# A transformer block on one core: chunk 0's first norm moved to ACT and POOL, and the last r and v products in high and low parts

## The reference

```python
x = x + attn(layernorm(x))        # causal linear attention, 16 heads of 16, features elu + 1
x = x + ffn(layernorm(x))
# attn: q = a @ Wq + bq; k, v = (a @ Wk + bk) @ Wc @ We, ...; o = num / den;
#       y = a + o @ Wo + bo;  return norm(y) * gamma + beta
# ffn:  xr = mu_r*x + (1-mu_r)*x_prev;  xk = mu_k*x + (1-mu_k)*x_prev
#       r = sigmoid(xr @ W_r);  k = xk @ W_k;  return r * (square(relu(k)) @ W_v)
```

## Time and profile before

| | us |
|---|---|
| median of 3 runs | 290.19 |
| lowest, highest | 287.93, 290.63 |
| profiled execution | 290.58 |
| its span, first to last instruction | 288.8 |
| PE busy | 264.8 (92%) |
| DVE busy | 225.1 (78%) |
| ACT busy | 154.1 (53%) |
| POOL busy | 127.3 (44%) |

### The profile page before, as it was taken

One profiled execution on the slowest core, in us unless ns is written; L12 is line 12 of the kernel. 1 busy time (PEld: TensorE's weight loads), 2 busy tenths in 40 slices (PEclk: granted clock), 3 DMA queues, 4 the chain that ended last, 5 costly groups with the idle time before them and its releaser, 6 DMA issues.

```text
span 288.8 us, 7520 instructions
## 1 busy us (share of the span) xinstructions
PE 264.8 (92%) x2961; PEld 190.6 (66%) x2961; DVE 225.1 (78%) x550; ACT 154.1 (53%) x312; POOL 127.3 (44%) x151
## 2 busy tenths in 40 slices
PE   7886988983899999999999999999999999989794
PEld 6755656742685588757885588558855767766563
DVE  6587487969597979977997989796979758977523
ACT  2384684480643866388456854586248630453540
POOL 2628423100983358515853576355543514051510
PEclk9998999996599999999999999999999999999999
DMA  7900120000020003000400020001000020000312
GB/s 195 265 19 11 65 76 3 2 0 2 4 72 0 2 24 123 2 5 2 145 2 2 0 76 2 0 2 64 13 2 3 1 74 2 0 2 1 109 36 73
DMA packets 12178, 10.73 MB, mean 37 GB/s; under 512 B 2288, under 2 KB 12144, under 8 KB 12144
## 3 DMA queue, kind: packets, MB, share of 16 engines
q1 hardware_dynamic: 11392, 9.97, 11.1%
q10 hardware_dynamic: 752, 0.30, 0.4%
HBM read 6.07 MB, written 4.19 MB: 36 GB/s over the span
## 4 chain that ended last, share of the span: by engine, by line
PE 77%; DVE 11%; ACT 5%; issue 3%; DMA 2%; POOL 1%; ACTq 0%; DVEq 0%; POOLq 0%
PE ps_x L461 10%; PE ps_x L381 9%; PE ps_z L432 6%; PE ps_x L476 6%; PE ps_x L483 6%; PE ps_x L375 6%; PE ps_y L448 5%; PE ps_y L453 5%; PE ps_x L501 4%; PE ps_x L469 3%; PE ps_z L476 3%; PE ps_z L483 2%; DVE probs L991 2%; PE ps_x L368 2%; PE ps_z L415 2%
## 5 line engine op out<-in xcount | busy, mean ns | idle before, releaser
L991 DVE TENSOR_TENSOR probs<-ps_z,causal 128x1024 f32<-128x1024 f32 x32 | 38.7, 1211 | 6.3 <-PE ps_z L432 5.5
L461 PE MATMUL ps_x<-wo_sb,oT 128*128 128x256 f32 x128 | 29.6, 382 | 0.0
L381 PE MATMUL ps_x<-aT,wq_sb 128*128 128x512 f32 x60 | 27.8, 604 | 0.0
L278 POOL TENSOR_TENSOR out_tok<-tanh_r,x_tok 128x512 f32<-128x512 f32 x14 | 17.8, 1275 | 21.9 <-DVE tanh_r L1064 20.9
L461 PEld LDWEIGHTS ps_x<-wo_sb,oT 128*128 128x128 f32 x128 | 23.6, 190 | 3.8 <-issue 0.9
L248 POOL TENSOR_TENSOR abo_tok<-a_tok,bo_bc 128x1024 f32<-128x1024 f32 x8 | 18.9, 2361 | 16.3 <-issue 5.6
L255 POOL TENSOR_TENSOR xb_tok<-x_in,beta_bc 128x1024 f32<-128x1024 f32 x8 | 18.9, 2356 | 16.0 <-DVE x_tok L1037 16.0
L218 POOL TENSOR_TENSOR rstd<-rstd,neg_half 128x4 f32<-128x4 f32 x24 | 24.9, 1038 | 1.9
L448 PE MATMUL ps_y<-qf,state 32*32 32x128 f32 x512 | 20.9, 278 | 5.3 <-DVE oT L1005 4.7
L432 PE MATMUL ps_z<-qf,kfT 32*128 32x128 f32 x512 | 24.1, 304 | 1.4 <-ACT rden_bc L711 0.5
L263 POOL TENSOR_TENSOR prod<-qf,ksum 128x1024 f32<-128x1024 f32 x5 | 11.8, 2361 | 29.9 <-DVE ksum L962 29.9
(11 more groups left out here) (144 smaller groups left out, 623.6 us busy)
## 6 DMA issues: line engine op xcount, KB each, us to landing
x_in<-in_L_attn_x_dram SPq DMA_DIRECT2D x8, 512.0 KB, 4.2
out_dram<-out_tok SPq DMA_DIRECT2D x16, 256.0 KB, 2.1
xr<-in_L_attn_Wq_dram ACTq DMA_DIRECT2D x1, 256.0 KB, 4.0
xk<-in_L_ffn_W_r_dram SPq DMA_DIRECT2D x1, 256.0 KB, 4.8
xk<-in_L_ffn_W_k_dram SPq DMA_DIRECT2D x1, 256.0 KB, 5.0
xr<-in_L_ffn_W_v_dram SPq DMA_DIRECT2D x1, 256.0 KB, 5.5
wo_sb<-in_L_attn_Wo_dram SPq DMA_DIRECT2D x4, 64.0 KB, 5.0
bo_bc<-in_L_attn_bo_dram SPq DMA_DIRECT2D x1, 128.0 KB, 5.0
```

Of the source, the lines that this page charges most:

```text
L278: PL.tensor_tensor(out_tok[:, 2 * i:2 * i + 2, :], tanh_r[:, i].rearrange("p (b d) -> p b d", b=2), x2_tok[m % 3][:, 2 * i:2 * i + 2, :], ...
L381: last = mm(bk_[:, :], wq_sb[:, k, a, :], aT[:, k, :], start=(k == 0), stop=(k == KD - 1))
L461: last = mm(bk_[:, (b % 2) * D:(b % 2 + 1) * D], oT[m % 2][:, a, b, :], wo_sb[:, a, :], start=(a == 0), stop=(a == 1))
L991: V.tensor_tensor(probs[b % 2][:].rearrange("p g (r s) -> p g r s", s=HALF), ps_z[:, :, 0:2 * P].rearrange("p g (r s) -> p g r s", s=HALF) ...
```

## The change

In the first short steps:

- `denominator_terms` goes from DVE to POOL for chunks 1 and 2 (DVE keeps chunk 0's, as `prepare_denominators`), and PE's `denominators` and `outputs(c, 3)` change places.
- Chunk 0's `centre` and `second_residual` leave DVE. POOL makes `rstd1` and `nbias1`, ACT's `normalise_y` scales y in place, and POOL's `scale_residual` multiplies by gamma and adds `xb_tok`, eight operations of 128 x 256. DVE takes chunk 0's second statistics in two halves.
- POOL's `second_norm` and `add_beta` change places, and PE's wait for the reciprocal at the head of a step becomes a wait for `s_den`, the operation before it.

In the finale, r and v of chunks 5, 6 and 7 are made from parts. ACT makes the high parts (`high_xr`, and `channel_k` with its last argument true), POOL the low ones (`low_xr`, `low_ka`), and PE calls `mix_r_parts` and `mix_v_parts`. The weight `wrT` is split once, in step 0. DVE's `second_residual(7)` goes behind the two r shifts of chunk 6.

```diff
+            def scale_residual(m):
+                for b in range(NB + 1):
+                    if b < NB:
+                        pool.wait_ge(s_n1, b + 1)
+                        PL.tensor_tensor(y_tok[:, b, :], y_tok[:, b, :], gamma_bc[:], ALU.mult).then_inc(s_t, 1)
+                    if b:
+                        pool.wait_ge(s_t, b)
+                        PL.tensor_tensor(x2_tok[m % 3][:, b - 1, :], y_tok[:, b - 1, :], xb_tok[m % 2][:, b - 1, :],
+                                         ALU.add).then_inc(s_x2, 1)
...
+            def low_parts(parts, whole, high, value, done):
+                for k in range(KD):
+                    pool.wait_ge(high, value + k + 1)
+                    PL.tensor_tensor(flat(parts[1])[:, k * T:(k + 1) * T], whole(k),
+                                     flat(parts[0])[:, k * T:(k + 1) * T].bitcast(F32), ALU.subtract).then_inc(done, 1)
...
                     if m >= 0:
-                        first_norm(m)
-                        second_norm(m)
+                        scale_and_bias(m, mv1, neg_mean1, rstd1, nbias1, s_st1, s_rs1, s_nb1)
+                        scale_residual(m)
                     else:
                         pool.wait_ge(s_kf, 2 * n + 2)
                     add_bo(n)
-                    add_beta(n)
                     if m < 0:
+                        add_beta(n)
+                        pool.wait_ge(wr_split, 1)
+                        PL.tensor_tensor(wr_p[1][:], wrT[:], wr_p[0][:].bitcast(F32), ALU.subtract).then_inc(wr_split, 1)
+                    denominator_terms(n)
+                    if m >= 0:
+                        second_norm(m)
+                        add_beta(n)
+                    else:
                         pool.wait_ge(wv_split, 1)
                         PL.tensor_tensor(wv_p[1][:], wvT[:], wv_p[0][:].bitcast(F32), ALU.subtract).then_inc(wv_split, 1)
                 if f >= 0:
...
+            def low_xr(m):
+                pool.wait_ge(s_r_ps, 2 * m)
+                low_parts(xr_p, lambda k: xr[:, k].rearrange("p b t -> p (b t)"), s_xrh, 2 * (m - FIRST), s_xrl)
+
+            def low_ka(m):
+                pool.wait_ge(s_v_ps, 2 * m)
+                low_parts(ka_p, lambda k: k_act[:, k, :], s_kah, 2 * m, s_kal)
...
                 m, f = c - 1, c - 2
                 token_difference(f)
                 first_norm(m)
+                low_xr(f)
                 second_norm(m)
+                low_ka(f)
                 first_norm(c)
                 token_difference(m)
+                low_xr(m)
                 second_norm(c)
+                low_ka(m)
                 finish(f)
+                low_xr(c)
                 finish(m)
+                low_ka(c)
...
+            def mix_r_parts(m, i, bk_):
+                pe.wait_ge(s_xrh, 2 * (m - FIRST) + 2)
+                for b in (2 * i, 2 * i + 1):
+                    out = bk_[:, (b % 2) * D:(b % 2 + 1) * D]
+                    for k in range(KD):
+                        for part in range(2):
+                            mm(out, xr_p[0][:, k, b * P:(b + 1) * P], wr_p[part][:, k, :], start=(k == 0 and part == 0), stop=False)
+                    if b == 0:
+                        pe.wait_ge(s_xrl, 2 * (m - FIRST) + 2)
+                    for k in range(KD):
+                        last = mm(out, xr_p[1][:, k, b * P:(b + 1) * P], wr_p[0][:, k, :], start=False, stop=(k == KD - 1))
+                last.then_inc(s_r_ps, 1)
...
                     if m < 0:
                         pe.wait_ge(ffn_w_sb, 2)
                         ffn_weight(2, x1)
-                denominators(n)
+                if f >= 0:
+                    denominators(n)
                 outputs(c, 3)
+                if f < 0:
+                    denominators(n)
                 if f >= 0:
                     pe.wait_ge(wv_split, 2)
...
                 out_projection(c, 1, x0)
                 mix_k(f, 1, z1)
-                mix_r(f, 0, z2)
-                mix_r(f, 1, z3)
+                mix_r_parts(f, 0, z2)
+                mix_r_parts(f, 1, z3)
                 pe.wait_ge(s_zT, 2 * f + 2)
-                mix_v(f, 0, x1)
+                mix_v_parts(f, 0, x1)
                 pe.wait_ge(s_y, 2 * c + 2)
                 transpose_z(m, x0, x2)
                 pe.wait_ge(s_oT, 4 * c + 4)
-                mix_v(f, 1, ps_y)
+                mix_v_parts(f, 1, ps_y)
...
+            def normalise_y(m):
+                act.wait_ge(s_nb1, 2 * m + 2)
+                for b in range(NB):
+                    AC.activation(y_tok[:, b, :], y_tok[:, b, :], ACT.Identity, bias=nbias1[:, b:b + 1],
+                                  scale=rstd1[:, b:b + 1]).then_inc(s_n1, 1)
...
+            def high_part(parts, whole, ready, value, done, ks=range(KD)):
+                for k in ks:
+                    act.wait_ge(ready, value + k + 1)
+                    copy(flat(parts[0])[:, k * T:(k + 1) * T], whole(k)).then_inc(done, 1)
...
                 if f >= 0:
                     gate_r(f, 0, x1)
+                if c == 1:
+                    normalise_y(m)
                 double_keys(n)
+                if c == 0:
+                    act.wait_ge(ffn_w_sb, 1)
+                    copy(flat(wr_p[0]), flat(wrT)).then_inc(wr_split, 1)
...
+            def high_xr(m):
+                act.wait_ge(s_r_ps, 2 * m)
+                high_part(xr_p, lambda k: xr[:, k].rearrange("p b t -> p (b t)"), s_xr, 2 * m, s_xrh)
+
             def finale(c):
                 m, f = c - 1, c - 2
                 act.wait_ge(s_rb_ps, c + 1)
@@ -855,20 +927,23 @@
                 for b, bk_ in ((0, ps_y), (1, x2), (2, x0), (3, x1)):
                     copy(rden_bc[c % 2][:, b].rearrange("p a t -> p (a t)"), bk_[:, 0:2 * P]).then_inc(s_rb, 1)
                 shift_z(f, x0, x1)
-                channel_k(f, 0, z0)
-                channel_k(f, 1, z1)
+                high_xr(f)
+                channel_k(f, 0, z0, True)
+                channel_k(f, 1, z1, True)
                 gate_r(f, 0, z2)
                 gate_r(f, 1, z3)
                 normalise_z(m)
                 shift_z(m, x0, x2)
-                channel_k(m, 0, z0)
-                channel_k(m, 1, z1)
+                high_xr(m)
+                channel_k(m, 0, z0, True)
+                channel_k(m, 1, z1, True)
                 normalise_z(c)
...
-            def second_stats(m):
+            def second_stats(m, rows=range(NB)):
                 if m >= 1:
                     dve.wait_ge(s_nb2, 2 * m)
-                dve.wait_ge(s_x2, 4 * m + 4)
-                row_stats(x2_tok[m % 3], stats2, s_st2, 8 * m, range(NB))
-                row_means(stats2, mv2, s_st2, 8 * m)
+                dve.wait_ge(s_x2, 4 * m + rows[-1] + 1)
+                row_stats(x2_tok[m % 3], stats2, s_st2, 8 * m, rows)
+                if rows[-1] == NB - 1:
+                    row_means(stats2, mv2, s_st2, 8 * m)
...
                 divide(c, 0)
                 mask(c, 2)
                 queries(n, 0, x0)
+                if m >= 0:
+                    second_stats(m, (0, 1))
                 queries(n, 1, x1)
                 divide(c, 1)
                 states(n)
                 key_sums(n)
-                denominator_terms(n)
                 mask(c, 3)
-                if m >= 0:
-                    centre(m)
-                    second_residual(m)
                 divide(c, 2)
                 if m >= 0:
-                    second_stats(m)
+                    second_stats(m, (2, 3))
...
                 gate(f, 1, ps_y)
                 token_shift(m, 0, *for_k)
                 token_shift(m, 1, *for_k)
-                second_residual(c)
                 token_shift(m, 0, *for_r)
                 token_shift(m, 1, *for_r)
+                second_residual(c)
                 second_stats(c)
```

53 lines of the change are left out of this document (26 added, 27 removed).

## The result

| us | before | after |
|---|---|---|
| median (lowest to highest), 4 runs each | 290.22 (287.93 to 290.63) | 295.25 (294.17 to 296.25) |
| profiled execution | 290.58 | 296.17 |
| its span | 288.8 | 294.4 |
| ratio after/before, 95% interval | | 1.0184 (1.0121 to 1.0246) |

The account below looks back on a forecast made before the run. PE bounds 90 to 230 us outright, with free time in the second short step and the finale. Forecast: 290.6 − 5.0 (front) + 10.9 (finale) = 296.5, 296.1 as median, since the profiled execution lies 0.4 over it; range 288.0 to 300.5.

Parts of the forecast that it names:

- length 1, clock falls / stays: Step c=1's reciprocal spread to step c=2's output projection: 4.2 us off if PE's clock falls, 5.9 if not.
- PE idle at v(5): Finale, chunk 5: after four high products of v, PE waits 4.0 us for POOL's low ka.
- mix_k(6), mix_k(7) from the finale's start: Finale: PE starts these calls for chunks 6 and 7 later than before, by 5.6 and 10.2 us.
- finale, clock down / up in the gaps: Finale's added time: 11.6 us if PE's clock falls in its gaps, 9.2 if it stays up; 10.9 taken.
- The front: First short steps, chunk 0's first norm off DVE: earlier output projection, 5.0 us off, ends 4.2 and 5.9.
- the replay: Finale worked through on the earlier trace's times: stretched residual, late statistics, POOL's queue, PE gaps, clock fall; end +11.6 us.
- PE's own saving: Finale: twelve r and v calls in parts, 1.44 us each for 1.73, save 3.5 us of PE.
- B: Rival, finale: the parts stay hidden and the finale saves its 3.5 us, total 280.8; chance 0.08.
- C: Rival, finale: POOL and DVE do not hinder each other, PE gaps of 2.4 us, total 288.4; chance 0.20.
- D: Rival, finale: clock also falls before mix_k, so mix_k(6) and (7) run at 1.2 GHz, 299.7; 0.15 with E.
- E: Rival, front: POOL's 256-column operations cost 1.27 us, about half the front's gain goes, total 299; 0.15 with D.
- length 0: From the start to the spread of the reciprocals in step c=1; the forecast's sum has no term for it.

Follow-up runs that it names:

- front_only: Changed kernel with the finale's r and v back as float32 products, so only the first steps are changed: 283.01 us, ratio 0.9762 to the kernel before.
- tail_parts_dve: Changed kernel with only r and v of chunk 7 in parts, their low parts on DVE, the rest float32: 284.42 us, ratio 0.9831.
- experiment 3: Also spelled low_xr_after_x2: changed kernel with POOL's low parts of xr(5) and xr(6) waiting until the next chunk's second_residual is done: 290.0 us, ratio 1.0016.
- v_parts_only: Changed kernel with r of chunks 5 to 7 as float32 products, only v in parts: 288.7 us, ratio 0.9953.
- lows_on_dve: Changed kernel with all low parts of the finale, chunks 5 to 7, on DVE and none on POOL: 287.97 us, ratio 0.9944.
- tail_and_filler: tail_parts_dve with twenty unused products on PE in the gaps of steps 0, 1 and 2: 282.77 us, ratio 0.9768.
- finale_only: Changed kernel with the first steps of the kernel before (wrT still split), so only the finale is changed: 301.46 us, ratio 1.0427.
- r_parts_only: Changed kernel with v of chunks 5 to 7 as float32 products, only r in parts: 288.52 us, ratio 0.9927.
- late_parts_dve: Changed kernel with only v(6), r(7) and v(7) in parts, their low parts on DVE, the rest float32: 285.79 us, ratio 0.9861.

## Why the prediction was right

| step | forecast | measured |
|---|---|---|
| POOL's 128x256 operation | 0.73, pitch 0.68 | 0.73, pitch 0.69 |
| length 1, clock falls / stays | −4.2 / −5.9, taken −5.0 | −4.70 / −6.14 |
| `second_residual(6)` | 3.97 | 3.71 |
| PE idle at v(5) | 4.0 | 3.79, then 3.77 at v(6) |
| the other eight products of v's first call | 1.7 | 1.06, then 1.87 |
| z transposes behind it | 2.0 | 1.83 and 1.66 |
| mix_k(6), mix_k(7) from the finale's start | +5.6, +10.2 | +4.76, +9.00 |
| finale, clock down / up in the gaps | +11.6 / +9.2, taken +10.9 | +11.87 / +9.19 |

**The front** came as worked out, with its clock: the taken −5.0 lies between its two ends, and both ends were seen, in the changed kernel and in front_only, 0.2 to 0.5 us better than forecast each.

**The finale** followed the replay, every link of it: the stretched residual, the late statistics, the queue on POOL, the gap, the clock. The replay was 0.8 us too pessimistic for mix_k(6) and 1.2 for mix_k(7), since the residual was 0.26 us shorter and the clock fell later than I let it: the other eight products of v's first call in chunk 5 still ran at full speed, 1.06 us for 1.7. The end was 1.5 us too optimistic for chunk 7: from mix_k(7)'s start to the end 2.87 us were added, and 1.4 forecast. The rows show why: with a wait of 1.82 us for chunk 7's ka_low the clock fell once more, and twelve products at 0.216 us instead of 0.12 are 1.15 us. The two errors cancel by luck, and +11.87 stands beside a replay of +11.6.

**PE's own saving**, 3.5 us by twelve calls of 1.44 us for 1.73, was real and worth nothing in chunks 5 and 6: PE was waiting. In tail_parts_dve four calls, 1.2 us by the same figures, shortened the finale by 1.0; the ratios do not show it.

**The rivals.** B (hidden parts) is excluded by the gaps, C (no hindrance) by 3.71 against 1.67 and by experiment 3. C's gap of 2.4 us was counted from the end of r (253.9); from the end of the high products (254.4), as the 4.0 is, it is 1.9, and v_parts_only, where nothing stretches the residual, has 1.99. D (clock down in mix_k) did not happen in the changed kernel's profile, where both calls took 3.67 us; it did in four of the others (low_xr_after_x2, v_parts_only, lows_on_dve, tail_and_filler), one mix_k of 5.37 us each. E (POOL's small operation at 1.27) is excluded by 0.73.

**What the sum lacked** is length 0. Before's profiled execution had the clock at 0.55 from 26.5 to 30 us, after's had not, behind the same stretch (2.55 us of PE work in 22 to 26.5 us, 2.54 in after): −1.59 us that is the clock's and no edit's: finale_only, with the first steps of before, has a length 0 of 44.97 and a clock of 1.00 there. The sum by the parts is then −1.6 − 4.7 − 0.1 + 11.9 = +5.5. Without it the forecast, 296.5 for an execution like before's, would have met 297.8. The median lies 0.9 under the profiled execution, so that 296.1 against 295.25 is partly luck. In the two edited places together +5.9 was forecast and +7.2 came; length 0 hid the 1.3.

**Not tested.** DVE's `second_residual(7)` behind the r shifts was never run by itself; r_parts_only, v_parts_only and lows_on_dve keep it, front_only, late_parts_dve, tail_parts_dve and tail_and_filler do not. What it costs inside the 11.9 us is open.
